# Keys and values of 33 head pairs of the second cross-attention layer made ahead and kept in DRAM, four row normalisations on GpSimd, and a new order of steps, in an eight-part transformer kernel

## The reference

```python
# layer 1, attention: 16 heads of 64, context as keys and values
q, k, v = x @ Wq * inv_temp, ctx @ Wk, ctx @ Wv
scores = q @ k.T / 8                                  # (256, 256) per head
full = softmax(scores)
keep = scores >= (32nd largest score of the row)
attn = full * keep / (sum(full * keep) + 1e-8)
x = x + (attn @ v) @ Wo
# layer 1, feed-forward: rows and hidden values rounded to 8 bits
x = x + down(quant(silu(gate(quant(norm(x)))) * up(quant(norm(x)))))
# layer 2, attention: the same shapes, a plain softmax over all 256 keys
x = x + softmax(q @ k.T / 8) @ v @ Wout + bout
# layer 2, feed-forward: rows rounded to FP8, one 256x256 matrix
x = x + round8(norm(x)) @ W.T * scale + bias
```

## Time and profile before

| | |
|---|---|
| median of 3 runs | 3421.66 us (3420.59 to 3421.78) |
| the profiled execution | 3419.01 us |
| its span, first to last instruction | 3417.2 us |
| busy share of the span | PE 90%, DVE 78%, ACT 69%, POOL 59% |
| phase of layers 1 and 2 | from about 745 us to about 2925 us of the span |

### The profile page before, as it was taken

The page is one execution under the profiler, slowest core; times in us unless marked ns, Lnnn a source line. Parts: engine busy times, 40 slices in busy tenths (PEclk is TensorE's granted clock), DMA queues, the critical chain, the costliest instruction groups (busy, mean ns, idle before and its releaser), DMA issues.

```text
span 3417.2 us, 63899 instructions
## 1 busy us (share of the span) xinstructions
PE 3082.2 (90%) x19271; PEld 2153.1 (63%) x19271; DVE 2666.7 (78%) x9901; ACT 2371.1 (69%) x7266; POOL 2027.8 (59%) x4023
## 2 busy tenths in 40 slices
PE   8999947967789999999999999999999999798994
PEld 5666624535456666666666666676676666576783
DVE  5666555539999999999999999999999953455334
ACT  6777711107889999999999999999999965233121
POOL 5666502437767777777777777777777733104126
PEclk9999967988889999999999999999999999899998
DMA  3320042450000000000000000000000000101788
GB/s 126 103 68 20 7 164 64 115 153 30 7 7 4 5 7 5 4 7 5 5 7 5 4 7 5 4 7 5 4 8 1 4 4 1 41 22 50 230 274 292
DMA packets 115662, 161.01 MB, mean 47 GB/s; under 512 B 10195, under 2 KB 97004, under 8 KB 115180
## 3 DMA queue, kind: packets, MB, share of 16 engines
q1 hardware_dynamic: 102902, 131.74, 11.9%
q0 software_dynamic: 12288, 25.18, 2.7%
q10 hardware_dynamic: 128, 0.00, 0.0%
HBM read 107.72 MB, written 47.59 MB: 45 GB/s over the span
## 4 chain that ended last, share of the span: by engine, by line
DVE 46%; PE 24%; ACT 5%; issue 5%; POOL 3%; DMA 3%; POOLq 0%; SPq 0%; DVEq 0%; ACTq 0%
DVE s_W L1317 9%; DVE s_W L1321 7%; DVE s_W L1303 5%; DVE s_W L1299 4%; DVE s_W L1308 4%; DVE s_W L1334 3%; PE ps L1492 2%; DVE s_st L197 2%; PE ps L1513 2%; PE ps L1523 2%; PE ps L2605 1%; PE ps L2616 1%; DVE s_W L232 1%; PE ps L864 1%; PE ps L1470 1%
## 5 line engine op out<-in xcount | busy, mean ns | idle before, releaser
L1228 POOL TENSOR_SCALAR s_W<-s_W 128x256 f32<-128x256 f32 x512 | 595.3, 1163 | 60.8 <-ACT s_W L1396 13.1
L1317 DVE MATCH_REPLACE8 s_W<-s_W 128x256 f32<-128x256 f32 x1024 | 409.5, 406 | 0.0
L1321 DVE MAX8 s_W<-s_W 128x8 f32<-128x256 f32 x1024 | 379.1, 410 | 0.0
L1492 PE MATMUL ps<-s_W 64*128 64x256 f32 x2048 | 366.3, 435 | 12.0 <-DVE s_W L1609 5.8
L1232 POOL TENSOR_TENSOR s_W<-s_W 128x256 f32<-128x256 f32 x512 | 363.3, 730 | 20.5
L1504 PE MATMUL ps<-s_idf,s_W 128*128 128x128 f32 x2048 | 333.1, 286 | 33.9 <-ACT s_W L1413 33.0
L1504 PEld LDWEIGHTS ps<-s_idf,s_W 128*128 128x128 f32 x2048 | 228.3, 142 | 172.4 <-issue 134.6
L1513 PE MATMUL ps<-s_W 128*64 128x256 f32 x2048 | 286.1, 401 | 39.0 <-ACT s_W L1430 32.8
L1430 ACT ACTIVATE s_W<-ps 128x512 f32<-128x512 f32 x512 | 308.6, 603 | 10.6 <-PE ps L1504 5.4
L1422 ACT ACTIVATE s_W<-ps,s_W 128x256 f32<-128x256 f32 x512 | 237.5, 471 | 110.9 <-DVE s_W L1334 110.7
L1253 POOL TENSOR_SCALAR s_W<-s_W 128x256 f32<-128x256 f32 x512 | 248.8, 498 | 86.0 <-DVE s_W L1339 86.0
(11 more groups left out here) (393 smaller groups left out, 8067.8 us busy)
## 6 DMA issues: line engine op xcount, KB each, us to landing
s_RA<-in_L_expert SPq DMA_DIRECT2D x36, 514.0 KB, 5.2
s_W<-in_ctxT SPq DMA_DIRECT2D x64, 256.0 KB, 2.6
s_RC<-in_L_expert SPq DMA_DIRECT2D x18, 514.0 KB, 5.7
s_RC<-expert_in SPq DMA_DIRECT2D x31, 256.0 KB, 4.5
expert_in<-s_W SPq DMA_DIRECT2D x4, 1280.0 KB, 6.3
expert_out<-s_RB SPq DMA_DIRECT2D x20, 256.0 KB, 5.3
s_W<-in_ctx SPq DMA_DIRECT2D x16, 256.0 KB, 3.1
s_RB<-in_F1T SPq DMA_DIRECT2D x8, 512.0 KB, 3.9
```

The costliest lines, as they stand in the source:

```text
L1228: at.append(g.did(g.e.tensor_scalar(cm[:, h, :], sc[:, h, :], sm[:, 48 + 8 * h + 7:48 + 8 * h + 8], NEG, ALU.is_lt, ALU.mult)))
L1317: cut_at.append(v.did(v.e.match_replace(out=cut[:, h, :], in_to_replace=m8[rnd][h], in_values=cut[:, h, :], imm_value=-3e38)))
L1321: i = v.e.max(m8[rnd + 1][h], cut[:, h, :])
L1492: i = mm(out[:, h, 0:256], q[64 * h:64 * h + 64, :], k[64 * h:64 * h + 64, :], start=True, stop=not first)
```

## The change

33 of c2's 128 pairs get their keys and values early: pair 7 of batches 4 to 12, and all eight of batches 13, 14 and 15. While c1 runs alone, one such pair is made in each of slots 0 to 32. SP loads the batch's context (`early_fetch`, 12 loads of 256 KB), PE makes keys and values into one bank (`early`), ACT copies the bank to one of two 128x512 buffers, and SP stores it in DRAM (`keys_values`, 33 stores of 256 KB). When the pair's turn comes SP loads keys and values back (`load_k`, `load_v`, 33 each of 128 KB), `qk` makes only the queries, and `values` has nothing to do. c2's weights are therefore loaded before slot 0 (`weights` at -6.242), and PE reaches the first early pair at slot -0.429, just ahead of `c1.scores` of item 0 at slot -0.016.

The normalised rows of c1, f1, c2 and f2 are written by POOL and no longer by DVE (8 instructions of 128x256 a batch). All offsets in `TIMES` are new; `AFTER` stays 43.

```diff
+EARLY = {0: (7,), 1: range(8), 2: range(8), 3: range(8), 16: (), 15: (), 14: (), 13: ()}
...
+        self.early = [] if first else [8 * b + g for b in range(B) for g in range(8) if g in EARLY.get(B - b, EARLY[0])]
...
+        fetches = [((b,), 16 * b + at - 9 * (b < 2)) for b in range(B)]
...
+            steps[p + "early_fetch"] = [((j,), first[j]) for j in first]
+            steps[p + "early"] = [((i,), i) for i in range(len(self.early))]
+            steps[p + "load_k"] = steps[p + "load_v"] = [((m,), 2 * m + at) for m in self.early]
...
+        def early_fetch(j):
+            if j >= 2:
+                sp.wait_ge(sig("ep"), self.early_up_to(j - 1))
+            load_context(j % 2, self.batches[j])
+
+        def early(i):
+            sp.wait_ge(sig("ev"), i + 1)
+            sp.e.dma_start(self.kv_d[i], self.KV[i % 2]).then_inc(sig(f"es{i % 2}"), 16)
...
+        def load_k(m):
+            sp.wait_ge(sig("sp"), 2 * (m - 1))
+            sp.e.dma_start(self.KT[m % 2], kept(m)[:, 0:256]).then_inc(sig(f"lk{m % 2}"), 16)
+
+        def load_v(m):
+            sp.wait_ge(sig("pvp"), m - 1)
+            sp.e.dma_start(self.KV[m % 2][:, 256:512], kept(m)[:, 256:512]).then_inc(sig(f"lv{m % 2}"), 16)
...
+        def norm(b):
+            g.wait_ge(sig("xTp"), b)
...
+            for k in range(2):
+                c.normalise(g, self.XN[:, k, :], 2 * b + k).then_inc(sig("norm"), 1)
...
-            for k in range(2):
-                c.normalise(v, self.XN[:, k, :], 2 * b + k).then_inc(sig("norm"), 1)
...
+        def early(i):
+            if i >= 2:
+                s.wait_ge(sig(f"es{i % 2}"), 16 * (i // 2))
+            s.wait_ge(sig("ep"), i + 1)
+            s.e.activation(self.KV[i % 2], self.M[P, "early", i], ACT.Copy).then_inc(sig("ev"), 1)
...
+        def early(i):
+            b, g = self.early[i] // 8, self.early[i] % 8
+            j = self.batches.index(b)
+            bank, cx = enter((P, "early", i)), self.CX[j % 2]
+            t.wait_ge(c.sig(f"w{self.layer}"), 64)
+            t.wait_ge(sig(f"c{j % 2}"), 16 * (j // 2 + 1))
+            keys(bank[:, 0:256], cx, g)
+            keyed_values(bank[:, 256:512], cx, g).then_inc(sig("ep"), 1)
...
-    "pe": {"late": 0, "c1.turn_x": -3.56, "c1.qk": -1.45, "c1.scores": -0.03, "c1.turn": 4.09,
+    "pe": {"late": -6, "c1.turn_x": -2.597, "c1.qk": -1.176, "c1.scores": -0.016, "c1.turn": 4.243,
...
+           "c2.turn_x": -2.969, "c2.qk": -1.666, "c2.early": -0.429, "c2.scores": 0.022, "c2.values": 0.374,
...
-    "sp": {"late": 0, "reload": 0, "c1.fetch": -22.75,
-           "c2.fetch": -23.73,
-           "weights": 4},
+    "sp": {"weights": -6.242, "late": -6, "reload": 0, "c1.fetch": -5.671,
+           "c2.early_fetch": -2.166, "c2.fetch": -1.153, "c2.early": 1.789, "c2.load_k": 1.915, "c2.load_v": 4.126},
```

More of the change, by code:

```diff
@@ L1148, in sig, with late_ones, loads, early_up_to @@
         return self.c.sig(f"c{self.layer}_{name}")
+    def late_ones(self, m):
+        return m + 1 - sum(e <= m for e in self.early)
+    def loads(self, m):
+        return sum(e <= m and e % 2 == m % 2 for e in self.early)
+    def early_up_to(self, j):
+        return sum(e // 8 in self.batches[0:j] for e in self.early)
+    def context(self, b):
+        return self.sig(f"c{b % 2}"), 16 * (b // 2 + 1 + (len(self.batches) + 1 - b % 2) // 2)
     def steps(self):
@@ L1487, in scores @@
             t.wait_ge(sig("qk"), m + 1)
+            if m in self.early:
+                t.wait_ge(sig(f"lk{m % 2}"), 16 * self.loads(m))
             if first:
```

133 lines of the change are left out of this document (87 added, 46 removed), and 41 rows, old and new, of tables (EARLIER, TIMES).

## The result

The changed kernel took 3404.12 us as the median of 6 runs (3401.33 to 3410.93), the kernel before 3421.18 us beside it on the same chip (6 runs, 3420.23 to 3425.72). The ratio is 0.9951, with a 95% interval of 0.9939 to 0.9964. So the change is faster by 17 us, where the prediction had 42: the direction and the range (3350 to 3415) hold, the size does not. The profiled execution took 3405.55 us, with a span of 3403.7.

A forecast was written before the change was run, and what follows sets the result against it. DVE paces head and joint stretch; PE follows closely and paces the tail. 15.6 + 9 - 2 - 34 - 31 + 0.3 = -42.1 from 3419.0, plus 2.7, gives 3380 us; range 3350 to 3415.

The forecast's parts named there:

- Start, +15.6: Start: the first early pair waits for c2's weight DMAs and delays c1's first scores, +15.6 us, bounds 12 to 18.
- Head, +9 and -2: Head: PE's work with an early pair exceeds DVE's by 0.27 us a slot, +9; normalisation off DVE gives -2.
- the case of a clock that stays at 0.85: Head: PE's clock stays at 0.85, +33 against the sum; with some tail gain missing 3413 to 3425, chance 0.08.
- The slower rival: Head: early pairs not hidden, 33 of them cost 58 us; 3431, or 3488 at the half clock; chance 0.12.
- Normalisation off DVE, 46 us at 460 ns, given to POOL at 0.50: Joint stretch: 100 instructions of 460 ns leave DVE, 45.96 us; on POOL each takes 0.50 us, 1.16 at the far bound.
- Hidden: Joint stretch: POOL, 75% busy, takes the normalisation at 78% or 82% without delay, unless it stands in a wait.
- Joint stretch, -34: Joint stretch: the middle between 46 us if DVE alone binds and 22 if PE alone binds, -34.
- picture of two bounds: Joint stretch: DVE and PE are both nearly full; whichever is relieved alone hands over after some 40 us.
- Tail, -31: Tail: 20.5 pairs without keys and values save PE 39.8 us, of which 31 are counted; bounds 15 to 40.
- 5.2 to 5.6 named as a sign: Tail: pairs of c2 taking 5.2 to 5.6 us in the next profile would show the prediction right.
- The first rival: Tail and joint stretch: batch 15 waits some 16 us for f1's tiles, PE binds and joint gives 22; 3408, chance 0.22.
- DVE alone binds, early pairs free in the head: Joint stretch gives 46 us and the head costs 0 instead of 9: 3359, chance 0.15.

The follow-up runs named there:

- after_wfirst: The changed kernel with c2's four weight loads issued before the last two tiles of x: 3397.43 us, ratio 0.9938 to the kernel before.
- after_mult: The changed kernel with POOL only multiplying rows by the inverse root, mean subtraction left out in layers 1 and 2: ratio 0.9922 to the kernel before.
- new_early_none: The changed kernel with normalisation on DVE, replaced in layers 1 and 2 by a two-column clearing after each buffer's first use: ratio 0.9895 to the kernel before.
- before_again: The kernel before, unchanged, profiled again on another chip for its stages: joint stretch 1683.1 us.
- old_early_dve: The kernel before with the early pairs added, old order and normalisation on DVE kept: ratio 0.9993 to the kernel before.
- new_early_dve_b: Repeat of new_early_dve on another chip: ratio 1.0012 to the kernel before, joint stretch 1711.5 us.
- after_again: The changed kernel, unchanged, run again on another chip: ratio 0.9960 to the kernel before, joint stretch 1689.4 us.
- new_early_dve: The changed kernel with all four normalisations back on DVE, early pairs and new order kept: ratio 0.9992 to the kernel before.
- new_noearly_dve: The changed kernel without early pairs and with normalisation on DVE, so the new order alone: ratio 1.0042 to the kernel before.
- the two short runs: Early pairs in old and new order, DVE normalising only 16 of 256 columns in layers 1 and 2: ratios 0.9941 and 0.9984 to the kernel before.
- old_early_pool: The kernel before with early pairs and normalisation on POOL, but in the old order: ratio 1.0122 to the kernel before.
- after_newton: The changed kernel with POOL's refinement for f2 placed six slots later: 3408.29 us, ratio 0.9956 to the kernel before.

## Why the prediction was right and wrong

**Start, +15.6: right.** 14.5 measured, by the mechanism named: the early pair ahead of c1's first scores waits 10.81 us for a DMA. The last weights landed at 777.0 (issued at 762.02, 15.0 us), and PE went on at 778.26 with the context behind them, where the prediction had 776.9 and 777.6. after_wfirst takes 10 of the 14.5 away.

**Head, +9 and -2: wrong by 8 us, on the good side.** The head took 261.7 us against 262.7, with PE busy 235 of 262 us at a clock of 0.96 (0.85 before), so the case of a clock that stays at 0.85 did not come. Measured inside the new order, the early pairs cost 4.7 us with the normalisation on DVE (258.7 to 263.4) and nothing with it on POOL (262.3 to 261.7). The order decides whether the room is used: in the old order the same pairs cost 17 us, at the same clock of 0.96. The slower rival's mechanism was thus real, at 17 us where it had 58, and the new offsets removed it. (The prediction counts 34 slots, but there are 33 pairs; this is 0.3 us.)

**Normalisation off DVE, 46 us at 460 ns, given to POOL at 0.50: both sizes wrong.** Taken away from DVE, the joint stretch's 100 instructions free 25 us in the old order and 38 in the new one; with the clearings that stand in their place (100 at 60 ns) it is an estimated 31 and 44. The rest came back as longer times of other DVE instructions; in the old order the negation's row alone grew by 8.5 us. On POOL one takes 1.22 us. "Hidden" did not hold either. The changed kernel (1689.4 to 1691.1) and after_mult (1680.8) differ in POOL's instruction alone, 1.22 and 0.50 us, and are 9 to 10 us apart. new_early_none, with nothing on POOL and the clearings on DVE, has 1676.0, so that POOL's instructions cost the stretch 14 us or, with the clearings off, an estimated 20.

**Joint stretch, -34: this step failed.** It measured +7.5. The prediction worked it out from the load of two engines ("both bounds are nearly met at once"), put the new order at nothing without a reason, and took POOL's load to be hidden. The runs show both at a price: 19 to 34 us for the order, and 14 for POOL. The runs give this ledger of the stretch:

| step | joint | difference |
|---|---|---|
| before (before_again) | 1683.1 | |
| early pairs, old order (old_early_dve) | 1679.8 | -3.3 |
| the new order (new_early_dve_b) | 1711.5 | +31.7 |
| normalisation off DVE (new_early_none) | 1676.0 | -35.5 |
| the same on POOL (after, after_again) | 1690.3 | +14.3 |

The profiles stand on several chips. The same kernel differed by 3.1 us between two chips (new_early_dve and new_early_dve_b) and by 1.7 between two others (after and after_again). So a step is good to about 3 us, and the 3.3 of the early pairs are not told from zero. The step of the order is 24 us without the early pairs (new_noearly_dve), 32 in this table, 34 between the two short runs on one chip, and 19 between the two without the instruction.

The ledger depends on its own order too. Put in first, the early pairs are worth nothing, as DVE binds; with the normalisation already on POOL, in the new order, the same early pairs are worth 20.7 us. So the prediction's picture of two bounds was right there. That nine tenths of DVE's relief come through was measured only where PE had been relieved already. In the old order and without POOL's load both reliefs together gave 1683.1 - 1657.1 = 26 us, an estimated 32 with the clearings off: within the bounds of 22 to 46 that the prediction had, and near its 34. The sum of the two reliefs was fair; what was left out is what the change pays for them, an order in which DVE stands idle some 23 us more, and POOL's load.

Why then is the order new? In the old one, POOL's instructions cost 31 us in the joint stretch and 18 in the tail (old_early_pool), and the early pairs 17 in the head. With both parts in, the new order is better by 1710.6 - 1690.3 = 20 us in the joint stretch alone, and the kernel by 1.0122 against 0.9951 to 0.9960. The offsets fit this mix of work, and none of the parts gains alone with them: the order with neither part is 0.4% slower than before, with the early pairs alone 0.9992 to 1.0012, with POOL's part alone 1.0075.

**Tail, -31: right, a little small.** -35.6. A pair went from 7.18 to 5.43 us, within the 5.2 to 5.6 named as a sign; that is 1.75 of the 1.94 us that PE saved, times 20.5 some 36 us. The prediction had held back 9 of the 39.8, and 4 stayed out. The order has a small part in it: without early pairs the new one's tail is 174.9 to 176.1 against 177.8 to 179.5. In the old order the early pairs gave 29.1 (177.8 to 148.7), in the new one 32.5 (174.9 to 142.4). The first rival's wait of batch 15 for f1's last two tiles did not come: it wanted the tail 16 us longer than forecast.

**Rivals.** The time came near that of the first rival, 3408, but not by its mechanism: the tail did not wait, and the joint stretch grew by 7.5 us where it had 22 less. "DVE alone binds, early pairs free in the head" had 3359. The head's part of it holds in the changed kernel. DVE alone binds only as long as it carries the normalisation: then the early pairs give 3.3 us in the old order and nothing in the new one. None of the cases held the cost of the order.

**What stays open.** Why the new order lets DVE wait at f1's multiplication was only named, not taken away: no order that has the head and the tail of the new one and the joint stretch of the old one was tried. After after_newton's edit the long batches were shorter and the others longer, so such waits can shift when one offset is changed. Not run either: the kernel before with the step taken from DVE and no early pairs, which would say how much of DVE's relief PE lets through there. A further version would join after_wfirst with a POOL normalisation of 0.50 us; the subtraction of the mean would then have to come from elsewhere, and it wasn't tried. Of what was run and leaves nothing out, after_wfirst is the fastest: ratio 0.9938 (0.9925 to 0.9951) against 0.9960 (0.9947 to 0.9972) for the changed kernel on the same chip.

## What to carry to other kernels

When four engines are each 75 to 97% busy and work through orders written by hand, price the order as a term of its own by running the new order with none of the new work; here it was as large as either relief. Two reliefs of two engines near their bound are to be measured together as well as one at a time, since here the early pairs were worth nothing in the joint stretch alone and 20.7 us beside the other part. An instruction's recorded duration is not what its removal frees, since part of it can be a fixed cost or a stand-still beside another engine, and the next instruction may then stand still in its place; a run in which it is left out tells what is freed. Work is moved to an engine with room at the price that it has there, for exactly that operation, and at 75% busy this engine's longer instructions still came to delay the others.

## What the runs showed of the hardware

- POOL takes 1216 ns for subtract and multiply by two columns on 128x256, and 498 ns for a multiply by one column and a constant: 2.4 times as much for the same bytes. DVE took 0.40 us for the first where POOL was idle (14 times in new_early_dve_b, 1500 to 2500 us).
- A TENSOR_SCALAR on DVE takes longer beside some of POOL's instructions. Sorted by what POOL was in when the DVE instruction started, in 1500 to 2500 us: L207 of the kernel before (two values a row) took 169 ns with POOL idle (17 times), 269 in L1253 (7 times) and 603 in L1232 (8 times); L232 took 417 ns in L1228 (30 times), 574 in L1253 (8 times) and 584 in L1232, up to 870 (22 times). In the changed kernel the same L207 met the scaling (L1331) 29 times of 33, and took 394 ns on average; twice it met POOL's normalisation and took 172. The duration of a small DVE instruction thus goes with what it meets on POOL. Over the joint stretch this adds up to little: DVE's busy time in the new order was 4 to 9 us longer with the normalisation on DVE (1645.3 and 1650.7 against 1641.6), and 4 us shorter without it.
- A TENSOR_SCALAR of 16 columns was never shorter than 265 ns in the joint stretch (about 100 in each of three runs, with medians of 290 to 441), and one of 256 columns never shorter than 382 (six runs with the step on DVE). A sixteenth of the columns thus leaves some two thirds of the time.
- The granted clock in the head rose from 0.85 to 0.96 as PE's busy time went from 203 of 264 to 235 of 262 us. It went with the early pairs in both orders: 0.96 in old_early_dve, 0.88 in new_noearly_dve.
